# Group 0 of a fused embedding and CIN kernel: one unit unsplit, and three reorderings on ScalarE, TensorE and SyncE

## The chip, the cores and the metric

The kernel runs on one NeuronCore of one Trainium2 chip. The metric is the time of one execution on the device in microseconds (us); the time of a kernel is the median of its runs. The engines are TensorE (PE, matrix products into PSUM), VectorE (DVE), ScalarE (ACT), GpSimd (POOL) and SyncE (SP, which here only starts transfers). Each works through its own list of instructions in order, and they meet in semaphores.

## What is computed

```python
e = stack([tbl_f[ids[:, f]] for f in range(32)], axis=1)      # (512, 32, 64)
def cin(x, w0, b0, w1, b1):                                    # w: (128, channels)
    z = einsum('bhd,bfd->bhfd', x, x).reshape(B, 32*32, D)
    y = relu(einsum('bcd,oc->bod', z, w0) + b0)
    hidden, direct1 = y[:, :64], y[:, 64:]
    z = einsum('bhd,bfd->bhfd', hidden, x).reshape(B, 64*32, D)
    direct2 = relu(einsum('bcd,oc->bod', z, w1) + b1)
    return concatenate([direct1, direct2], axis=1).sum(-1)
h = concatenate([cin(e, ...), dense_ctx], axis=1)
y = relu(relu(h @ W_top1 + b_top1) @ W_top2 + b_top2) @ W_top3
```

All of it is float32. Almost all of the time goes into the two layers of the CIN: elementwise products of rows, then matrix products over them.

## The kernel before, in words

The 512 samples are worked in G = 64 groups of eight. A tile has 512 columns (8 samples x 64) and 128 partitions, a row of channels each. Work comes in units of four such tiles. Group g has one unit of layer 1, **P**, and four of layer 2, **A**, **C**, **B** and **D** (`LAYER_2`, L28). P of group g+1 is worked beside layer 2 of group g, so the order of products on VectorE is A(g), P(g+1), C(g), B(g), D(g) (`period`, L76).

A unit goes this way. VectorE multiplies rows of x (`xd` for P, A and C, `xe` for B and D, in the one buffer `xs`) by another operand (`px0` for P, and for layer 2 the PSUM tensor `hid`, whose slot 0 is the "straight" hidden rows, read by A and B, and slot 1 the "swapped" ones, read by C and D) into one of ZF = 5 slots of `zf` (`products`, L582; L616). Then `mode` (L35) says how TensorE takes it:

- whole ("F"): four float32 matrix products straight from `zf` (`main`, L717; eight records in the trace). Needs nothing of ScalarE or GpSimd.
- split ("P" or "V"): ScalarE rounds `zf` to fp32r, the high part `zh` (`high`, L434; L442); GpSimd (mode P, L377) or VectorE (mode V) subtracts it, which leaves the low part `zl` (`low`). TensorE makes eight products of the high part with the two parts of the weights (`main`, L725 and L726), and later four with the low part (`late`, L737). These are fp32r products.

P and D are whole, A of group 0 and of the odd groups below 11 too; C is split, in group 0 by mode P. Which weights are kept whole, split or both is in `WHOLE_NAMES` and `SPLIT_NAMES` (L96); they are turned and copied once, before the first group, on TensorE, ScalarE (L416 to L423) and VectorE. From group 11 on one tile of some units goes by a PSUM bank of its own (`through_bank`, L50); that is no part of this change.

What orders the work is written out by hand, one loop over the groups for each engine:

- **TensorE** (L782): main A(g), late B(g-1), main P(g+1), the small product that ends layer 1 (`tail`, L756), late A(g), then main C(g), main B(g), main D(g), late C(g).
- **ScalarE** (L513): high A(g); `high_s` and `copy_x0(g+2)` (L432, from the landed `x0` into `px0`); high C(g); `finish_2(g-1)` (relu of layer 2); high B(g); then `finish_straight(g+1)` (L466 and L467: the straight `hid` of the next group, which VectorE's A(g+1) waits for; it waits for the tail of P(g+1) and for VectorE's product of B(g), which reads the old one), `finish_dir1`, `finish_swapped`.
- **VectorE** (L658): products of A(g), in odd groups a sum (L647), products of P(g+1), a small one (`products_s`), C(g), `low_s`, B(g), D(g).
- **GpSimd** (L382): low A(g), a gather, low C(g), a gather, low B(g), a gather. The gathers (L366) bring later samples' embeddings; before the loop GpSimd issues the first 32 of them.
- **SyncE** (L337): starts `load_xt(g+2)` (L307), `load_x0(g+3)` (L301), `load_xd(g+2)` (L318), a store of gathered rows to DRAM (L284), `load_xe(g+1)` (L324). Each load is four transfers; x0 and xt bring 256 KB in all, xd and xe 1 MB each. `load_x0(k)` waits for `copy_x0(k-1)`, `load_xd(k)` for VectorE's product of C(k-2), `load_xe(k)` for that of D(k-1).

The waits name positions (`NTH`, `NTH_SPLIT`, `NTH_WHOLE`), which are counted from `mode`, so they follow a unit whose mode changes. `closing(g)` (L108) says which unit of a group is the last to be added up.

Of the kernel before, what the change touches and what calls it, by code (L numbers as in the profile page):

```python
# [13 lines left out]
P = 128  # L14
B, F, D = 512, 32, 64
# [4 lines left out]
G = B // NS  # L20
# [13 lines left out]

def mode(unit):  # L35
    name, g = unit
    if name in "PD" or unit == ("A", 0):
        return "F"
    if g == LAST and name != "A":
        return "F" if name == "B" else "V"  # L40
    if name == "A" and g < 11 and g % 2:
        return "F"
    if name == "C" and g < 11:
        return "P" if g % 2 or g == 0 else "V"
    return "P"


# [2 lines left out]
def through_bank(unit):  # L50
    name, g = unit
    return name == "P" and g > 43 or name == "C" and 11 <= g < 43 or name == "D" and 11 <= g < LAST
# [18 lines left out]
def batch_of(g):  # L71

    return len(FIRST_BATCHES) + g if g < len(LATER_BATCHES) else None
# [19 lines left out]
OWN = "PD"  # L93
NTH_OWN = {u: i + 1 for name in OWN for i, u in enumerate(v for v in BANKED if v[0] == name)}
NTH_LOW = {u: i + 1 for m in "PV" for i, u in enumerate(LOW[m])}
WHOLE_NAMES = "PABD"  # L96
SPLIT_NAMES = "ACB"


def slot(u):  # L100
    return (NTH[u] - 1) % ZF


def split_slot(u):
    return (NTH_SPLIT[u] - 1) % ZS
# [14 lines left out]
def dlrm_tower(nc, dense_ctx, ids, tables, W_top1, b_top1, W_top2, b_top2, W_top3, w0, b0, w1, b1,  # L120
               eye, out):
    with ExitStack() as ctx:
        def sb(name, shape, dt=F32):
            return ctx.enter_context(nc.sbuf_tensor(name, shape, dt))
# [10 lines left out]
        wl = sb("wl", [P, len(SPLIT_NAMES), T, P], F32R)  # L135
        wf = sb("wf", [P, len(WHOLE_NAMES), T, P])
        whB = sb("whB", [P, len(OWN), P], F32R)
# [113 lines left out]
        def _(sp):  # L251
# [38 lines left out]
            def run_of_rows(k, r):  # L290
                src = rows(k, r)
                return bass.AP(tensor=src.tensor, offset=src.offset, ap=[[P * D, F], [1, N]])


            def load_x0(k):
                if k % GC == 0:
                    sp.wait_ge(x_stored[k // GC], 16 * STORES[k // GC])
                if k >= 2:
                    sp.wait_ge(x0_ready, k - 1)
                for j in range(4):  # L300
                    sp.dma_start(x0[F * j:F * j + F], run_of_rows(k, 0)).then_inc(x0_in, 16)  # L301

            def load_xt(k):
                if k >= 2:
                    sp.wait_ge(s_mult, k)
                for j in range(4):
                    sp.dma_start(xt[F * j:F * j + F], run_of_rows(k, 16)).then_inc(xt_in, 16)  # L307
# [6 lines left out]
            def load_xd(k):  # L314
                if k >= 2:
                    sp.wait_ge(mult, NTH["C", k - 2])
                for j in (0, 2, 1, 3):
                    sp.dma_start(xd[k % 2][F * j:F * j + F], block_rows(k, j, 0)).then_inc(xd_in[k % 2], 16)  # L318

            def load_xe(k):  # L320
                if k >= 1:
                    sp.wait_ge(mult, NTH["D", k - 1])
                for j in (0, 2, 1, 3):
                    sp.dma_start(xe[F * j:F * j + F], block_rows(k, j, T)).then_inc(xe_in, 16)  # L324
# [12 lines left out]
            for g in range(G):  # L337
                if g + 2 < G:
                    load_xt(g + 2)
                if g + 3 < G:  # L340
                    load_x0(g + 3)
                if g + 2 < G:
                    load_xd(g + 2)
                if g >= 1 and batch_of(g - 1) is not None:
                    store_batch(batch_of(g - 1))
                if g + 1 < G:
                    load_xe(g + 1)
# [47 lines left out]
        def _(act):  # L395
# [20 lines left out]
            for b, name in enumerate("PACBD"):  # L416
                act.wait_ge(w_turned, b + 1)
                if name in WHOLE_NAMES:
                    act.activation(wf[:, WHOLE_NAMES.index(name)].rearrange("p t n -> p (t n)"), banks[b], ACT.Copy).then_inc(w_high, 1)
                if name in SPLIT_NAMES:  # L420
# [13 lines left out]
            def high(u):  # L434
                if mode(u) == "F":
                    return
                s, q, i = slot(u), split_slot(u), NTH_SPLIT[u]
                act.wait_ge(mult, NTH[u])
                if i > ZS:
                    act.wait_ge(used_split, i - ZS)  # L440
                first = 1 if through_bank(u) else 0
                act.activation(zh[:, q, first:T], zf[:, s, first:T], ACT.Copy).then_inc(hi, 1)  # L442
# [17 lines left out]
            def finish_straight(k):  # L460
                act.wait_ge(y1_ready, k + 1)
                if k >= 1:
                    act.wait_ge(mult, NTH["B", k - 1])
                else:
                    act.wait_ge(w_low, 5)
                act.activation(hid[0:H, 0], py1[0:H], ACT.Relu, bias=bias0[0:H]).then_inc(straight, 1)  # L466
                act.activation(hid[H:P, 0], py1[0:H], ACT.Relu, bias=bias0[0:H]).then_inc(straight, 1)  # L467
# [23 lines left out]
            def finish_2(g):  # L491
                need_used(act, closing(g))
                act.activation(py2[:, g % 2], py2[:, g % 2], ACT.Relu, bias=bias1[:]).then_inc(dir2_ready, 1)  # L493
# [19 lines left out]
            for g in range(G):  # L513
                high(("A", g))
                if g + 1 < G:
                    high_bank(("P", g + 1))
                    high_s(g + 1)
                    if g + 2 < G:
                        copy_x0(g + 2)
                high_bank(("C", g))  # L520
                high(("C", g))
                if g % GC == GC - 1:
                    place_sums_1(g // GC)
                if g >= 1:
                    finish_2(g - 1)
                high(("B", g))
                if g + 1 < G:
                    finish_straight(g + 1)
                    high_bank(("D", g))
                    finish_dir1(g + 1)  # L530
                    finish_swapped(g + 1)
# [12 lines left out]
        def _(dve):  # L544
# [18 lines left out]
            for b, name in enumerate("PACBD"):  # L563
                done += (name in WHOLE_NAMES) + (name in SPLIT_NAMES) + (name in OWN)
                if name in OWN:
# [113 lines left out]
        def _(pe):  # L679
# [15 lines left out]
            def bank(u):  # L695
                return py1[:] if u[0] == "P" else py2[:, u[1] % 2]

            def main(u):
                name, g = u
                s, y, first = slot(u), bank(u), name in "PA"  # L700
                if name == "P" and g >= 1:
                    pe.wait_ge(swapped, 3 * g)
                    pe.wait_ge(dir1_ready, g)
                if name == "A" and g >= 2:
                    pe.wait_ge(sum2_done, g - 1)
                if mode(u) == "F":
                    ends = name != "P" and closing(g) == u
                    w = WHOLE_NAMES.index(name)
                    if u != ("P", 0):
                        pe.wait_ge(mult, NTH[u])  # L710
                    first_tile = 1 if through_bank(u) else 0
                    for h in range(first_tile, T):
                        if u == ("P", 0) and h < T - 1:
                            pe.wait_ge(first_tiles, h + 1)
                        elif u == ("P", 0):
                            pe.wait_ge(mult, 1)
                        mm = pe.matmul(y, wf[:, w, h], zf[:, s, h], start=first and h == first_tile, stop=ends and h == T - 1)  # L717
                    mm.then_inc(used_whole, 1)
                else:
                    q, w = split_slot(u), SPLIT_NAMES.index(name)  # L720
                    pe.wait_ge(hi, NTH_SPLIT[u])
                    if through_bank(u):
                        pe.wait_ge(bank_hi, NTH_BANKED[u])
                    for h in range(T):
                        pe.matmul(y, wh[:, w, h], zh[:, q, h], start=first and h == 0, stop=False)  # L725
                        pe.matmul(y, wl[:, w, h], zh[:, q, h], start=False, stop=False)  # L726
# [55 lines left out]
            for g in range(G):  # L782
                main(("A", g))
                if g >= 1:
                    late_own(("D", g - 1))
                    late(("B", g - 1))
                if g + 1 < G:
                    main(("P", g + 1))
                    main_own(("P", g + 1))
                    late_own(("P", g + 1))  # L790
                    tail(g + 1)
                late(("A", g))
                main(("C", g))
                main(("B", g))
                main(("D", g))
                late(("C", g))
                main_own(("D", g))
            late(("B", LAST))
# [44 lines left out]
```

## Time and profile before

| | before |
|---|---|
| median of 3 runs | 1066.68 us (1065.88 to 1066.71) |
| profiled execution | 1065.6 us |
| its span | 1063.8 us |
| TensorE busy | 1017.4 us (96%) |
| VectorE busy | 948.7 us (89%) |
| GpSimd busy | 921.4 us (87%) |
| ScalarE busy | 772.5 us (73%) |

The span is the time from the first to the last instruction in the trace; 1.8 us of the profiled execution lie around it. Times in the views count from the start of the span. The first 62 us are the start (weights turned, first embeddings gathered, written to DRAM and loaded back), the 64 groups take the time from there to about 1038 us at some 15.2 to 16 us each, and the last layers the rest.

### The profile page before, as it was taken

Reading aid. Unit: us, or ns where it says so; the run is one execution under the profiler, and the core shown is the slowest. Engines: PE = TensorE matmul, PEld = TensorE weight load, DVE = VectorE, ACT = ScalarE, POOL = GpSimd, SP = SyncE. Lnnn points to the kernel's source line nnn. Section 1 sums busy time; section 2 is a strip of 40 time slices with the busy share of each in tenths; the row PEclk is TensorE's granted clock in tenths of the full one; section 3 lists DMA queues with packets and bytes.
Section 4 is the critical chain, followed back from the end, with each engine's and each line's share of the span. In section 5 each row is a group of like instructions: output and inputs, shape, how many; then the busy total and the mean of one; then the engine's idle time right before and its main releaser. Section 6 shows DMA issues by size and latency. Waiting matters only on the chain.

```text
span 1063.8 us, 11316 instructions
## 1 busy us (share of the span) xinstructions
PE 1017.4 (96%) x3523; PEld 662.5 (62%) x3523; DVE 948.7 (89%) x777; ACT 772.5 (73%) x908; POOL 921.4 (87%) x311
## 2 busy tenths in 40 slices
PE   2389999999999999999999999999999999999999
PEld 1146656666666666666666666666766666666663
DVE  3069999999999999999999999999999999999991
ACT  5057666678778877887788778877887787788772
POOL 6538878899999999999999999999998899899880
PEclk9999999999999999999999999999999999999999
DMA  6488788778778877887788778877766776777630
GB/s 172 97 204 193 183 194 188 179 188 192 179 180 197 185 184 181 192 194 182 182 189 189 183 177 195 192 184 172 177 168 163 168 183 163 165 181 179 162 79 0
DMA packets 140638, 183.92 MB, mean 173 GB/s; under 512 B 55633, under 2 KB 56273, under 8 KB 140450
## 3 DMA queue, kind: packets, MB, share of 16 engines
q1 hardware_dynamic: 135986, 178.93, 69.9%
q0 software_dynamic: 4096, 4.20, 2.7%
q8 instruction: 28, 0.46, 0.2%
q14 instruction: 32, 0.26, 0.1%
q10 hardware_dynamic: 496, 0.06, 0.0%
HBM read 174.66 MB, written 8.39 MB: 172 GB/s over the span
## 4 chain that ended last, share of the span: by engine, by line
PE 63%; DVE 15%; issue 9%; POOL 4%; DMA 3%; ACT 3%; SPq 2%; POOLq 0%; DVEq 0%; ACTq 0%
PE py L717 27%; PE py L737 11%; PE py L725 11%; PE py L726 11%; DVE zf L616 10%; POOL emb L366 3%; DMA xs<-x_dram 3%; DVE zlB L636 2%; DVE pzS L625 1%; ACT hid L467 1%; DVE zS L629 1%; ACT hid L466 1%; PE py L756 1%; POOL zl L377 1%; PE py L752 1%
## 5 line engine op out<-in xcount | busy, mean ns | idle before, releaser
L377 POOL TENSOR_TENSOR zl<-zf,zh 128x2048 fp32r<-128x2048 f32 x179 | 790.0, 4418 | 84.8 <-ACT zh L442 82.3
L616 DVE TENSOR_TENSOR zf<-xs,hid 128x2048 f32<-128x2048 f32 (+1 forms) x256 | 539.5, 2109 | 36.4 <-ACT hid L467 30.6
L717 PE MATMUL py<-zf,wf 128*128 128x512 f32 x936 | 423.2, 592 | 2.1 <-DVE zf L616 2.1
L442 ACT ACTIVATE zh<-zf 128x2048 fp32r<-128x2048 f32 x185 | 340.0, 1838 | 93.4 <-DVE zf L616 92.7
L725 PE MATMUL py<-zh,wh 128*128 128x512 f32 x740 | 292.3, 395 | 3.9 <-ACT zh L442 3.5
L726 PE MATMUL py<-zh,wl 128*128 128x512 f32 x740 | 290.6, 393 | 0.0
L717 PEld LDWEIGHTS py<-zf,wf 128*128 128x128 f32 x936 | 176.8, 189 | 175.1 <-issue 161.0
L737 PE MATMUL py<-zl,wh 128*128 128x512 f32 x740 | 228.7, 431 | 1.4 <-POOL zl L377 1.4
L737 PEld LDWEIGHTS py<-zl,wh 128*128 128x128 f32 x740 | 139.3, 188 | 67.5 <-issue 37.8
L725 PEld LDWEIGHTS py<-zh,wh 128*128 128x128 f32 x740 | 139.5, 188 | 42.2 <-issue 7.8
L726 PEld LDWEIGHTS py<-zh,wl 128*128 128x128 f32 x740 | 139.6, 189 | 30.0
L366 POOL DMA_INDIRECT emb<-in_tbl,idx x128 | 131.2, 1025 | 28.7 <-issue 22.9
L616 DVE TENSOR_TENSOR zf<-xs,px 128x2048 f32<-128x2048 f32 (+1 forms) x63 | 133.0, 2112 | 4.6 <-issue 4.0
L458 ACT ACTIVATE zS<-pzS 128x512 fp32r<-128x512 f32 x64 | 38.4, 599 | 86.7 <-DVE pzS L625 86.7
L493 ACT ACTIVATE py<-py,bias 128x512 f32<-128x512 f32 x64 | 42.0, 656 | 24.5 <-PE py L737 23.3
L615 DVE TENSOR_TENSOR pzB<-xs,hid 128x512 f32<-128x512 f32 x84 | 57.7, 687 | 0.0
L466 ACT ACTIVATE hid<-py,bias 64x512 f32<-64x512 f32 x64 | 41.0, 641 | 21.1 <-PE py L756 21.0
L652 DVE TENSOR_REDUCE zsum<-py 128x8 f32<-128x512 f32 x64 | 43.7, 683 | 8.4 <-ACT py L493 8.4
L636 DVE TENSOR_TENSOR zlB<-pzB,zhB 128x512 fp32r<-128x512 f32 x72 | 49.2, 684 | 0.0
L629 DVE TENSOR_TENSOR zS<-pzS,zS 64x512 fp32r<-64x512 f32 x64 | 44.5, 695 | 2.6 <-ACT zS L458 0.7
L473 ACT ACTIVATE dir<-py,bias 64x512 f32<-64x512 f32 x64 | 43.9, 686 | 1.6
L486 ACT ACTIVATE hid<-py,bias 32x512 f32<-32x512 f32 x64 | 41.1, 643 | 3.9 <-DVE zf L616 2.4
(100 smaller groups left out, 611.2 us busy)
## 6 DMA issues: line engine op xcount, KB each, us to landing
xs<-x_dram SPq DMA_DIRECT2D x512, 256.0 KB, 5.3
xs<-x_dram SPq DMA_DIRECT2D x504, 64.0 KB, 2.1
x_dram<-emb SPq DMA_DIRECT2D x66, 64.0 KB, 5.6
x_dram<-emb SPq DMA_DIRECT2D x22, 96.0 KB, 5.3
emb<-in_tbl,idx POOLq DMA_INDIRECT x128, 4.8
x_dram<-emb SPq DMA_DIRECT2D x4, 384.0 KB
xs<-in_L_rec_w SPq DMA_DIRECT2D x2, 512.0 KB, 4.4
xs<-in_L_rec_w SPq DMA_DIRECT2D x1, 1024.0 KB, 6.9
```

Source lines behind the costliest of these rows:

```text
L366: pool.indirect_dma_start(out=emb[:, c % 2, f, :], out_offset=None, in_=tables[f], in_offset=bass.IndirectOffsetOnAxis(ap=idx[:, c, f:f + ...
L377: pool.tensor_tensor(zl[:, q, first:T], zf[:, s, first:T], zh[:, q, first:T].bitcast(F32), ALU.subtract).then_inc(lo["P"], 1)
L442: act.activation(zh[:, q, first:T], zf[:, s, first:T], ACT.Copy).then_inc(hi, 1)
L466: act.activation(hid[0:H, 0], py1[0:H], ACT.Relu, bias=bias0[0:H]).then_inc(straight, 1)
L615: dve.tensor_tensor(pzB[:], left[:, 0], view(right, at, [[1, N]]), ALU.mult).then_inc(bank_mult, 1)
L616: dve.tensor_tensor(zf[:, slot(u), first:T], left[:, first:T], view(right, at, [[0, T - first], [1, N]]), ALU.mult).then_inc(mult, 1)
L629: dve.tensor_tensor(zS[H:P], pzS[H:P], zS[H:P].bitcast(F32), ALU.subtract).then_inc(s_lo, 1)
L636: dve.tensor_tensor(low_part, pzB[:], high_part.bitcast(F32), ALU.subtract).then_inc(bank_lo, 1)
L717: mm = pe.matmul(y, wf[:, w, h], zf[:, s, h], start=first and h == first_tile, stop=ends and h == T - 1)
L725: pe.matmul(y, wh[:, w, h], zh[:, q, h], start=first and h == 0, stop=False)
L726: pe.matmul(y, wl[:, w, h], zh[:, q, h], start=False, stop=False)
L737: mm = pe.matmul(y, wh[:, w, h], zl[:, q, h], start=False, stop=ends and h == T - 1)
```

## The change

In group 0 only: C is made whole, ScalarE finishes the straight `hid` of group 1 ahead of B's high part, TensorE takes D ahead of B, and SyncE starts `load_xd(2)` ahead of `load_x0(3)`. C's weights are kept whole beside their split form, for which `wf` grows by one name (2 KB in each partition) and ScalarE makes one more copy at the start.

```diff
 def mode(unit):
     name, g = unit
-    if name in "PD" or unit == ("A", 0):
+    if name in "PD" or unit in (("A", 0), ("C", 0)):
         return "F"
@@
     if name == "C" and g < 11:
-        return "P" if g % 2 or g == 0 else "V"
+        return "P" if g % 2 else "V"
@@
-WHOLE_NAMES = "PABD"
+WHOLE_NAMES = "PABCD"
@@ SyncE
                 if g + 2 < G:
                     load_xt(g + 2)
+                if g == 0:
+                    load_xd(g + 2)
                 if g + 3 < G:
                     load_x0(g + 3)
-                if g + 2 < G:
+                if 0 < g < G - 2:
                     load_xd(g + 2)
@@ ScalarE
+                if g == 0:
+                    finish_straight(1)
                 high(("B", g))
                 if g + 1 < G:
-                    finish_straight(g + 1)
+                    if g > 0:
+                        finish_straight(g + 1)
                     high_bank(("D", g))
                     finish_dir1(g + 1)
@@ TensorE
                 main(("C", g))
-                main(("B", g))
-                main(("D", g))
+                for name in "DB" if g == 0 else "BD":
+                    main((name, g))
                 late(("C", g))
```

## Rows read from the trace of the kernel before

**Rows 1.** The page: busy us (share of the span) x instructions, by engine.
```profile
PE 1017.4 (96%) x3523; PEld 662.5 (62%) x3523; DVE 948.7 (89%) x777; ACT 772.5 (73%) x908; POOL 921.4 (87%) x311
```

**Rows 2.** The chain that ended last, whole run: start us, us, what.
```profile
712.28 3.43 PE py L717 x8
717.41 1.19 DVE zf L616
```

**Rows 3.** The same chain from 44 to 110 us.
```profile
69.08 0.60 ACT px L432
69.69 1.84 ACT zh L442
...
80.51 0.93 PE py L737 x4
81.44 3.43 PE py L717 x8
...
89.46 0.23 PE py L725
```

**Rows 4.** Timeline of TensorE: start us, us, line, operation [idle before <- releaser].
```profile
62.39 7.13 PE L717 MATMUL py<-zf,wf 128*128 128x512 f32 x16 [2.15 <-DVE zf L616]
...
68.96 0.80 PE L756 MATMUL py<-zS,wS 128*128 128x512 f32 x1
...
71.57 0.50 PE L725 MATMUL py<-zh,wh 128*128 128x512 f32 x1 [1.81 <-ACT zh L442]
```

**Rows 5.** Three windows: engines' busy us (x), PEclk, DMA share, GB/s.
```profile
69.50:71.50 2.00, 0.25 (x2) 0.00 (x0) 2.00 (x2) 2.00 (x3) 0.00 (x0) 1.00 0.26 61
72.50:75.50 3.00, 3.00 (x9) 2.32 (x8) 1.19 (x2) 2.92 (x5) 3.00 (x1) 0.50 0.85 206
77.50:81.50 4.00, 4.00 (x13) 2.12 (x12) 1.91 (x2) 0.00 (x0) 4.00 (x1) 1.00 0.98 235
```

**Rows 6.** Timeline of ScalarE, groups 0 and 1.
```profile
69.62 3.70 ACT L442 ACTIVATE zh<-zf 128x2048 fp32r<-128x2048 f32 x2
...
73.22 0.63 ACT L466 ACTIVATE hid<-py,bias 64x512 f32<-64x512 f32 x1
...
73.88 0.65 ACT L467 ACTIVATE hid<-py,bias 64x512 f32<-64x512 f32 x1
...
87.77 1.91 ACT L442 ACTIVATE zh<-zf 128x2048 fp32r<-128x2048 f32 x1 [0.58 <-DVE zf L616]
```

**Rows 7.** Timeline of VectorE, groups 0 and 1.
```profile
68.34 4.49 DVE L616 TENSOR_TENSOR zf<-xs,hid 128x2048 f32<-128x2048 f32 x2
...
74.63 2.29 DVE L616 TENSOR_TENSOR zf<-xs,hid 128x2048 f32<-128x2048 f32 x1 [1.81 <-ACT hid L467]
...
76.84 0.68 DVE L647 TENSOR_REDUCE sums<-dir 128x8 f32<-128x512 f32 x1
...
79.61 2.29 DVE L616 TENSOR_TENSOR zf<-xs,px 128x2048 f32<-128x2048 f32 x1 [2.09 <-issue]
...
85.45 2.29 DVE L616 TENSOR_TENSOR zf<-xs,hid 128x2048 f32<-128x2048 f32 x1
```

**Rows 8.** Timeline of SyncE's queue: the starts for x0 of 3 and xd of 2.
```profile
69.71 1.70 SPq L301 DMA_DIRECT2D xs<-x_dram  x4
71.45 1.85 SPq L318 DMA_DIRECT2D xs<-x_dram  x4
```

**Rows 9.** Timeline of GpSimd, group 0: the low part of C.
```profile
71.60 4.58 POOL L377 TENSOR_TENSOR zl<-zf,zh 128x2048 fp32r<-128x2048 f32 x1 [26.38 <-ACT zh L442]
```

**Rows 10.** Timeline ahead of the loop: TensorE's wait, GpSimd's gather of batch 4.
```profile
41.77 5.24 PE L770 MATMUL py<-wf 128*128 128x512 f32 x8 [21.68 <-DMA emb<-in_tbl,idx]
...
44.27 0.94 POOL L366 DMA_INDIRECT emb<-in_tbl,idx  x1 [0.30 <-issue]
```

**Rows 11.** The chain ahead of the loop: the last store of batch 3.
```profile
46.72 2.16 DMA x_dram<-emb
```

**Rows 12.** Waits of VectorE, 717 to 1020 us: total us, times, longest us.
```profile
DVE pzB L615 <- DMA xs<-x_dram: 2.7, 2, 1.5
```

## The prediction

> **What bounds the kernel now.** I began with the busy times on the page: TensorE is busy for 96% of the span [rows 1], more than any other engine, so time is to be had only where TensorE stands still or runs slowly, or where the chain leaves it. The chain that ended last says where that is. It runs on TensorE's products from 77 us to 712.28 us without a break by another engine, and goes over to VectorE at 717.41 us [rows 2]. Ahead of that, in group 0, it runs over ScalarE: the copy of x0 of group 2 at 69.08, then C's high part from 69.69 to 71.53, then TensorE [rows 3]. TensorE's own timeline shows the same from its side: A and P without a pause from 62.39, the tail recorded at 68.96 for 0.80 (so ended at 69.76), and then 1.81 us of idle until C's high part is there, at 71.57 [rows 4]. The windows show a second loss behind the idle: the granted clock is 0.50 between 72.5 and 75.5 us, so 1.2 instead of 2.4 GHz, and 1.00 before and after [rows 5].
>
> How much is lost there in all comes from the ends of the tail and of group 1's A. The tail ends at 69.76 and A of group 1 ends at 81.44 + 3.43 = 84.87 [rows 3, 4], which is 15.11 us. At full speed the work between them is C main 8 x 0.23 = 1.84, B main 1.84, D 3.43, late C 0.93 and A 3.43, or 11.47 us (0.93 and 3.43 are the entries at 80.51 and 81.44, 0.23 a small product such as that at 89.46) [rows 3]. So 3.64 us are lost: the 1.8 of idle, and 1.8 of slow clock.
>
> From 82 us on TensorE has no gap, so what it gains by then is carried on. I take it to be carried to the end, also behind 717 us: VectorE's work there hangs on semaphores of the other engines and not on a date, and everything in it moves together.
>
> **C unsplit.** TensorE needs C's product only, and not its high part. That product is made directly ahead of the small `low_s` and B's at 68.34 [rows 7], so it is ready at about 67.6 while TensorE gets to it at 69.76. The idle goes. The price is 3.43 for a whole unit instead of 1.84 + 0.93 = 2.77, so 0.66 us more of TensorE. ScalarE loses a high part of 1.84 [rows 3], GpSimd a low part of 4.58 [rows 9]; neither is the bound here.
>
> **D ahead of B on TensorE.** C then ends at 69.76 + 3.43 = 73.19. D's product ends at 68.34 + 4.49 = 72.83 [rows 7], 0.36 before; D ends at 76.62. If B came first, it would need its high part. ScalarE now does the straight hid first: it needs B's product (half-way through the entry of 4.49, so at 70.6) and the tail (69.76), starts at 70.65, and by the two durations of 0.63 and 0.65 [rows 6] ends at 71.95. B's high part follows and ends at about 73.85, 0.7 us after C's end at 73.19. The order D, B hides that. B main ends at 76.62 + 1.84 = 78.46. Late C is gone. A of group 1 ends at 78.46 + 3.43 = 81.89.
>
> So the sum of TensorE's part is 84.87 - 81.89 = **2.98 us** (3.64 lost before, less 0.66).
>
> **Straight hid first on ScalarE.** VectorE's A of group 1 waited 1.81 us for it and began at 74.63 [rows 7]. It now begins when D's product is over, at 72.9, and ends 2.21 later at 75.1. TensorE wants it at 78.46, so this is not on the path by itself; it starts the row of what follows. What is queued behind the moved step on ScalarE is B's high part (73.85 instead of 73.32, wanted at 76.62) and then `finish_dir1` and `finish_swapped`, which end at about 76.5. Of GpSimd, B's low part now starts at 73.9 and takes 4.58 [rows 9], so it ends at 78.5; TensorE wants it at 81.89.
>
> **xd of 2 ahead of x0 of 3.** VectorE's P of group 2 began at 79.61 after 2.09 us with no releaser named [rows 7]. The sum ahead of it had ended at 77.5, and what it needs beside that is xd of group 2, whose first transfer started at 71.45 [rows 8]; from there to its use are 8.16 us. The load waits only for C's product, so it now starts at 67.6. At the same 8.16 us it is used at 75.8, which is just when VectorE is through with A and the sum (75.1 + 0.68). I expect it sooner, as 256 KB of x0 no longer lie ahead of it and the DMA engines were at 0.26 of their time between 69.5 and 71.5 us [rows 5]. The four starts take 1.85 us [rows 8], to 69.5, and x0 of 3 has to wait for the copy that ends at 69.68 anyway: it starts at 69.7 as before, but its data come behind the 1 MB. Its use is the copy behind group 1's small product, at about 79.5; it has ten us. xe of 1 waits for D's product (72.83) and starts then; before, it followed xd's starts, at 71.45 + 1.85 = 73.3, so it is 0.5 us sooner.
>
> Then VectorE's chain in group 1 is: P of 2 at 75.8, B of 1 another 85.45 - 79.61 = 5.84 later [rows 7], at 81.65, its product ended at 83.9 and its high part, by 1.91 [rows 6], at 85.8. TensorE wants that at 91.30 - 2.98 = 88.3 (before, C began at 89.46 and took 1.84). The lead is 2.5 us. Without this reordering P would stay at 79.6, the high part at 87.77 + 1.91 = 89.68 [rows 6], and TensorE would stand for 1.4 us. So this part brings nothing by itself, and saves 1.4 of the 2.98.
>
> Here a rule speaks against the simple reading of the queue. The Trainium skill says, in "DMA: Bandwidth & Descriptors", section "Two DMAs through the same engine are not ordered", that in one queue descriptors start in order but are pipelined, and that nothing orders transfers across the 16 engines. By it xe of 1 may run beside xd of 2 and delay it, up to the case without any gain from the reordering. The rows leave this open: the DMA engines were at 0.98 from 77.5 to 81.5 us [rows 5], when parts of both loads were under way.
>
> **The start.** One more copy of weights on ScalarE, about 0.6 us, lies under the 21.68 us in which TensorE waits for gathers [rows 10]; without that cover it would cost its 0.6. On GpSimd the second gather of batch 4 stood behind C's low part. With that gone it is issued right behind the first one (44.27, 0.94 each) [rows 10], at about 45.5, beside the last stores to DRAM that the chain runs through (46.72, 2.16 us) [rows 11]. Bounds: 0 if it slips into the gaps, 2.2 if the stores had to wait until it is through, as long as a store takes. It is 32 KB on another queue than the stores', so I take 0.1, near the lower end.
>
> **Sum:** 2.98 - 0.1 = 2.9 us. Against the profiled execution, 1065.6 - 2.9 = 1062.7 us; the median of the runs is 1.1 us above that execution, so the forecast for the median is **1063.8 us**. A measurement of this kernel can tell about 0.2%, 2.1 us, from no change; 2.9 is 0.27%.
>
> **Rivals.**
>
> 1. The slow clock stays. The granted clock fell after 1.81 us of idle [rows 4, 5], but 2.15 us of idle lie ahead of A at 62.39 [rows 4] and stay as they are; the clock held through the 16 records behind it (7.13 us, so 0.43 us apart as in 3.43 for eight). If the dip is still there, it falls on C and D and costs its 1.8: gain 1.1, time 1065.6. The Trainium skill, "TensorE: Matmul & The Clock Gate", "Part 1: The HAM clock gate", has the clock follow how busy TensorE has lately been and its change vary from run to run, so by that rule a dip could also come of the earlier gap. For my forecast: with the change there is no idle from 62.39 on. Chance 0.08.
> 2. A transfer takes back the gain. xd of 2 or xe of 1 does not come sooner, and TensorE waits in group 1 for B's high part: gain 2.98 - 1.4 = 1.6, time 1065.1. For it: xe of 1 starts only 0.5 us sooner. Against: 2.5 us of lead. Chance 0.12.
> 3. Slower. From 717 us on VectorE sets the pace and has no slack; a load that lands late there is paid in full. Twice it was: 2.7 us, the longest 1.5 [rows 12]. The change starts loads in another order and moves all phases by 3 us. If four more loads out of some twenty groups come late, each by 1.35, the kernel loses 5.4 - 2.9 = 2.5, time 1069.2; from the third late one on (4.05) it is slower than before, from the fourth by over 0.2%. Against it: the order of loads differs in group 0 only. Chance 0.04. The same in the other direction, those 2.7 us going away, gives 1061.1; chance 0.03.
> 4. The gather at the start hits the stores in full: gain 0.8, time 1065.9. Chance 0.03.
>
> That the change doesn't do what it says I rule out nearly: the waits are counted from the modes.
>
> **How the numbers follow.** The forecast has the remaining 0.70. Its own range is 1063.1 to 1064.6, by the 0.4 or so to which the runs agree and some tenths of the sum. The range for 8 in 10 takes in rivals 1 and 2: 1062.8 to 1065.6. Faster by over 0.2% means a gain over 2.1 us: nearly all of the forecast's cases (0.67), the better end of rival 2 (0.02) and the lucky case (0.03), 0.72. Slower by over 0.2% only by rival 3: 0.04. Within 0.2%: the rest, 0.24.
>
> **What would show it.** In the trace after: TensorE at L717 without an idle entry from 62.4 on, through C and D of group 0 to about 76.6; PEclk at 1.00 in the window 72.5 to 75.5; A of group 1 ended at about 81.9; VectorE's A of 1 at 72.9 and P of 2 at about 75.8, with no wait for a transfer over some tenths; and in the later groups the same times less 3 us, such as the chain leaving TensorE at about 714 us. An idle entry of TensorE before B of group 1 speaks for rival 2, a PEclk of 0.5 near 73 us for rival 1, more than 3 us of VectorE waiting for transfers after 714 us for rival 3, and a first A later than 62.4 for rival 4.

## The result and the profile after

The changed kernel takes 1062.28 us as the median of 6 runs (1060.93 to 1062.75), the kernel before 1066.28 in 6 runs beside it (1064.68 to 1066.94): ratio 0.9968, 95% interval 0.9955 to 0.9980. The forecast was 1063.8 us, 2.9 us less than before; the two medians differ by 4.0 us, the ratio says 3.4, and its interval 2.1 to 4.8 us less. In absolute terms the median lies 0.5 us below the prediction's range of 1062.8 to 1065.6. That range counted from the 1066.68 us of the first three runs, and the kernel before measured 1066.28 in the six; 1066.68 x 0.9968 is 1063.3, which lies inside. The profiled execution took 1062.44 us with a span of 1060.6 us, against 1065.6 and 1063.8, so 3.2 us less.

The page of the changed kernel, busy times and the granted clock by slices: TensorE is busy for as long as before (1017.4), in a span that is 3.2 us shorter.

```profile
PE 1017.3 (96%) x3519; PEld 661.0 (62%) x3519; DVE 947.4 (89%) x777; ACT 770.0 (73%) x908; POOL 917.9 (87%) x310
...
PEclk9999999999999999999999999999999999999999
```

The chain of the changed kernel from 44 to 110 us (start, duration, what) in place of [rows 3]: from A of group 0 at 62.16 everything is TensorE's; the 16 records from 69.53 are C and D, and A of group 1 ends at 78.43 + 3.43 = 81.86.

```profile
62.16 7.13 PE py L723 x16
...
69.53 7.06 PE py L723 x16
...
78.43 3.43 PE py L723 x8
```

TensorE's timeline, where [rows 4] had 1.81 us of idle ahead of C: there is no idle entry, C and D begin 0.63 us after the tail.

```profile
62.16 7.13 PE L723 MATMUL py<-zf,wf 128*128 128x512 f32 x16 [1.23 <-DVE zf L622]
68.73 0.80 PE L762 MATMUL py<-zS,wS 128*128 128x512 f32 x1
69.36 7.22 PE L723 MATMUL py<-zf,wf 128*128 128x512 f32 x16
...
78.27 3.60 PE L723 MATMUL py<-zf,wf 128*128 128x512 f32 x8
```

Three windows, as [rows 5] (the last three columns are PEclk, DMA share, GB/s): the clock is at 1.00 where it was at 0.50, and the DMA engines are at work between 69.5 and 71.5 us.

```profile
69.50:71.50 2.00, 2.00 (x6) 0.82 (x5) 2.00 (x2) 0.75 (x2) 0.00 (x0) 1.00 0.89 210
72.50:75.50 3.00, 3.00 (x8) 1.25 (x7) 3.00 (x3) 2.92 (x4) 1.54 (x1) 1.00 1.05 239
77.50:81.50 4.00, 4.00 (x14) 2.13 (x12) 3.80 (x4) 2.06 (x3) 2.94 (x3) 1.00 0.73 194
```

ScalarE, VectorE, SyncE and GpSimd, as [rows 6 to 10]. ScalarE makes the straight hid at 70.72, then B's high part. VectorE's entry of 6.68 us holds B, D and A of group 1 in one, without the wait of 1.81; P of group 2 starts at 75.54 without a wait, 7.93 us behind the first start of its load. In the eight traces in which P of 2 does wait, from 7.94 us (g1) to 9.22 us (f2) lie between the two, against the 8.16 us of the prediction. SyncE starts xd of 2 at 67.61, x0 of 3 at 69.48, xe of 1 at 72.85. GpSimd issues the second gather of batch 4 at 45.58.

```profile
70.72 0.65 ACT L469 ACTIVATE hid<-py,bias 64x512 f32<-64x512 f32 x1 [1.27 <-DVE zf L622]
71.40 0.65 ACT L470 ACTIVATE hid<-py,bias 64x512 f32<-64x512 f32 x1
71.98 1.90 ACT L445 ACTIVATE zh<-zf 128x2048 fp32r<-128x2048 f32 x1
...
83.96 1.91 ACT L445 ACTIVATE zh<-zf 128x2048 fp32r<-128x2048 f32 x1 [0.47 <-DVE zf L622]
```

```profile
68.34 6.68 DVE L622 TENSOR_TENSOR zf<-xs,hid 128x2048 f32<-128x2048 f32 x3
74.94 0.68 DVE L653 TENSOR_REDUCE sums<-dir 128x8 f32<-128x512 f32 x1
75.54 2.28 DVE L622 TENSOR_TENSOR zf<-xs,px 128x2048 f32<-128x2048 f32 x1
...
81.64 2.29 DVE L622 TENSOR_TENSOR zf<-xs,hid 128x2048 f32<-128x2048 f32 x1 [0.30 <-DMA xs<-x_dram]
```

```profile
67.61 1.74 SPq L318 DMA_DIRECT2D xs<-x_dram  x4
69.48 1.86 SPq L301 DMA_DIRECT2D xs<-x_dram  x4
72.85 1.74 SPq L324 DMA_DIRECT2D xs<-x_dram  x4
```

```profile
45.58 0.94 POOL L369 DMA_INDIRECT emb<-in_tbl,idx  x1 [0.30 <-issue]
73.96 4.57 POOL L380 TENSOR_TENSOR zl<-zf,zh 128x2048 fp32r<-128x2048 f32 x1 [27.44 <-ACT zh L445]
```

The chain over the whole run leaves TensorE at 714.39 instead of 717.41 [rows 2], and the waits of VectorE behind it for transfers are what they were [rows 12].

```profile
709.26 3.43 PE py L723 x8
714.39 1.19 DVE zf L622
```

```profile
DVE pzB L621 <- DMA xs<-x_dram: 2.8, 2, 1.8
```

### The profile page after: what moved, and what is told of

It reads as the page before. It is cut to its first block, busy times and chain, and to the rows that moved or that the text cites. A ratio compares the mean times of both kernels' runs of the same rounds, so it can differ in the third digit from the quotient of the medians.

```text
span 1060.6 us, 11306 instructions
## 1 busy us (share of the span) xinstructions
PE 1017.3 (96%) x3519; PEld 661.0 (62%) x3519; DVE 947.4 (89%) x777; ACT 770.0 (73%) x908; POOL 917.9 (87%) x310
## 4 chain that ended last, share of the span: by engine, by line
PE 64%; DVE 16%; issue 9%; ACT 4%; DMA 2%; ACTq 2%; SPq 1%; POOL 1%; POOLq 0%; DVEq 0%
PE py L723 28%; DVE zf L622 11%; PE py L743 11%; PE py L731 10%; PE py L732 10%; DVE zlB L642 2%; DMA xs<-x_dram 1%; ACTq L502 1%; DVE pzS L631 1%; ACT hid L470 1%; DVE zS L635 1%; ACT hid L469 1%; PE py L762 1%; POOL zl L380 1%; DMA xs<-in_L_rec_w 1%
## 5 line engine op out<-in xcount | busy, mean ns | idle before, releaser
L445 ACT ACTIVATE zh<-zf 128x1536 fp32r<-128x1536 f32 (+1 forms) x184 | 338.2, 1838 | 94.5 <-DVE zf L622 90.5
L631 DVE TENSOR_TENSOR pzS<-xs,px 128x512 f32<-128x512 f32 x63 | 43.4, 689 | 0.0
```

What stands on the lines that cost most here:

```text
L631: dve.tensor_tensor(pzS[:], left, right, ALU.mult).then_inc(s_mult, 1)
```

## The experiments

To read them, three stretches of the profiled executions are told apart. The tail (the small product that ends layer 1, one for each group) marks the groups on TensorE's timeline. From the tail of group 4 to that of group 45 the traces all take 625.5 us (625.7 in e4, 626.1 in the second trace of the changed kernel); what differs is the first groups and the last ones.

| kernel | A of 0 starts | tail of 2 | tail of 4 | tail of 4 less A of 0 | P of 2 on VectorE | slow clock (0.50) from |
|---|---|---|---|---|---|---|
| before | 62.39 | 88.67 | 120.09 | 57.70 | 79.61 | 72 |
| changed | 62.16 | 85.66 | 117.07 | 54.91 | 75.54 | none |
| changed, second trace (f1) | 62.41 | 85.98 | 117.40 | 54.99 | 75.86 | none |
| e1: C unsplit alone | 62.60 | 87.02 | 120.82 | 58.22 | 81.16 | none |
| e2: C unsplit and xd | 62.83 | 87.83 | 119.24 | 56.41 | 77.18 | 63 |
| e3: without xd | 63.28 | 89.57 | 120.99 | 57.71 | 79.93 | 62.5 |
| e4: without D first | 63.37 | 88.46 | 119.87 | 56.50 | 76.98 | 64 |
| e5: xd alone | 63.04 | 87.63 | 119.05 | 56.01 | 77.93 | none |
| e6: three orders, C split | 62.56 | 87.23 | 118.65 | 56.09 | 76.03 | none |
| e7: C's idle filled | 62.60 | 88.65 | 120.07 | 57.47 | 80.15 | 63 |
| f2: changed, A's idle filled | 62.37 | 85.67 | 117.09 | 54.72 | 76.84 | none |
| f3: before, A's idle filled | 62.78 | 89.11 | 120.56 | 57.78 | 80.89 | 73 |
| f4: as f2, without xd | 62.34 | 85.79 | 119.67 | 57.33 | 79.92 | none |
| g1: before, both filled | 62.03 | 86.40 | 118.27 | 56.24 | 78.63 | none |

The slow clock meant in the last column is the one in the first groups. It turned out to be there in some executions and not in others, and the mean granted clock of each timed run tells which: without it the mean is 1.000 or 0.989, with it 0.997 or 0.998, or 0.986 or 0.987. What lies between 1.000 and 0.989 is another stretch at 0.50, of some 24 us, ahead of the groups; of the kernels with and without it, g1 and f2 (busy us of TensorE, x, PEclk, DMA share, GB/s):

```profile
24.00:27.00 3.00, 0.00 (x0) 1.00 0.66 128
```

```profile
24.00:27.00 3.00, 0.00 (x0) 0.50 0.68 136
```

Of 112 runs of the kernel before, 50 have the slow clock in the first groups. Of these, 39 have a mean of 0.986 or 0.987, and 11 one of 0.997 or 0.998. In the six traces that have it, the first pair of values goes with a slow clock behind the idle ahead of A (e2, e3, e4, e7), the second with one behind C's idle (before, f3). So the place that the forecast had read from one trace is, by this sign, the rarer one. The sign is not a proof: e2 and e3, which have no idle ahead of C, have one run each at 0.998, and f3, which has none ahead of A, one at 0.987.

**e1: only C unsplit.**

```diff
-    if name in "PD" or unit == ("A", 0):
+    if name in "PD" or unit in (("A", 0), ("C", 0)):
         return "F"
-        return "P" if g % 2 or g == 0 else "V"
+        return "P" if g % 2 else "V"
-WHOLE_NAMES = "PABD"
+WHOLE_NAMES = "PABCD"
```

> Only C of group 0 made whole; the three orders are as before. Theory (my account of the forecast): TensorE goes on from the tail into C without idle; B's high part now follows the copy of x0 and VectorE's product of B (70.6), so it ends at about 72.5, before C ends at 73.2, and neither straight-first nor D-first is needed. A of group 1 ends 2.98 us sooner than before (about 81.9 us in the trace), but P of group 2 still waits for xd until 79.6, and TensorE then idles about 1.4 us before B of group 1: gain 1.6 us, ratio 0.9985. Rival (the gain is spread over the parts, the straight hid being the wait that counts): VectorE's A of group 1 starts only at about 73.9, A of group 1 on TensorE is late, and the gain at its end is under 2 us and under 1 us in all.

Measured: 1066.03 us against 1065.98, ratio 1.0001 (0.9992 to 1.0010). No gain at all, less than even the 1.6 us of the theory. VectorE's P of group 2 and the idle entries of TensorE in this kernel:

```profile
81.16 2.29 DVE L616 TENSOR_TENSOR zf<-xs,px 128x2048 f32<-128x2048 f32 x1 [3.78 <-issue]
```

```profile
83.59 3.67 PE L717 MATMUL py<-zf,wf 128*128 128x512 f32 x8 [0.45 <-DVE zf L616]
...
88.24 0.50 PE L725 MATMUL py<-zh,wh 128*128 128x512 f32 x1 [0.72 <-ACT zh L442]
...
91.29 0.50 PE L725 MATMUL py<-zh,wh 128*128 128x512 f32 x1 [0.93 <-ACT zh L442]
...
104.37 1.20 PE L737 MATMUL py<-zl,wh 128*128 128x512 f32 x4 [0.21 <-POOL zl L377]
```

P of 2 waits for its load until 81.16, not 79.6 (in this execution the starts on SyncE were later too), and TensorE then waits four times. The tail of 2 came 1.65 us sooner than before, the tail of 4 at 120.82, 0.73 later. In this execution what C unsplit saves is all given back to a load.

**e2: C unsplit and xd ahead of x0.** As e1, and

```diff
+                if g == 0:
+                    load_xd(g + 2)
                 if g + 3 < G:
                     load_x0(g + 3)
-                if g + 2 < G:
+                if 0 < g < G - 2:
                     load_xd(g + 2)
```

> C of group 0 whole and xd of 2 ahead of x0 of 3; ScalarE's and TensorE's orders as before. Theory: these two parts make the whole gain: A of group 1 ends at about 81.9, P of group 2 starts on VectorE at about 76.8, no idle entry on TensorE in group 1: gain 3.0 us, as much as the whole change, within 0.5 us of it. Rival (the straight hid first or D first has a part): over 1 us less gain than the whole change.

Measured: 1063.15 us, ratio 0.9974 (0.9965 to 0.9983), 2.8 us less than before. The whole change has 0.9968 and 0.9969; the intervals overlap, and half a microsecond between them can't be excluded. No idle entry in group 1. But the trace has the slow clock behind the idle ahead of A of group 0, in a place where the trace before did not have it. The windows (busy, x, PEclk, DMA share, GB/s), and TensorE's A and P of group 0 in it, 8.83 instead of 7.13 us:

```profile
60.00:63.00 3.00, 0.61 (x3) 1.00 1.07 240
63.00:66.00 3.00, 3.00 (x5) 0.56 1.05 231
66.00:69.00 3.00, 3.00 (x8) 0.87 1.00 228
```

```profile
62.83 8.83 PE L719 MATMUL py<-zf,wf 128*128 128x512 f32 x16 [2.39 <-DVE zf L618]
```

Less these 1.7 us, tail of 4 less A of 0 is 54.7, as in the changed kernel. The times show the same cost: the four runs of e2 with the slow clock have a median of 1064.62 us, the seven without it 1063.05, which is 2.2 us less than the 14 runs of the kernel before without it on the same chip (1065.26).

**e3: without the reordering on SyncE.** The change with load_xd where it was.

> The change without the reordering on SyncE. Theory: A of group 1 still ends 3.0 us sooner, P of group 2 starts at 79.6 as before, B's high part of group 1 is late and TensorE idles about 1.4 us ahead of B of group 1: gain 1.6 us, as in the kernel with C unsplit alone. Rival (the load would have come in time anyway, xe of 1 sets the pace): full gain of 3.0 us. Second rival: the delay is felt in later groups too and grows past 1.4: gain under 1 us.

Measured: 1066.22 us, ratio 0.9994 (0.9983 to 1.0004). The trace could not judge the theory: P of 2 was late as foreseen (79.93), but a slow clock from 62.5 us on, to 69.3, twice as long as in the other traces, had put TensorE 3 us back (10.12 instead of 7.13 us for the first 16 records), so that it met no late product.

```profile
63.28 10.12 PE L720 MATMUL py<-zf,wf 128*128 128x512 f32 x16 [2.82 <-DVE zf L619]
```

By the median of all runs the gain of the change is gone but for 0.6 us. Six of the eleven runs have the slow clock (median 1066.34); the five without it have a median of 1063.77, 1.5 us less than the kernel before without it, near the 1.6 of the theory. Five runs that spread over 3.8 us can't decide this; f4 below has it with twelve.

**e4: without D ahead of B.**

```diff
-                for name in "DB" if g == 0 else "BD":
-                    main((name, g))
+                main(("B", g))
+                main(("D", g))
```

> The change without D ahead of B on TensorE. Theory: B's high part, behind the straight hid on ScalarE, ends at about 73.9 and C at about 73.0 to 73.2, so TensorE idles 0.7 to 0.9 us before B of group 0: A of group 1 ends 0.7 to 0.9 us later than in the changed kernel, gain about 2.2 us. The clock stays at 1.00, since the idle is short. Rival: the idle is enough to bring the slow clock back: gain under 1 us.

Measured: 1064.04 us, ratio 0.9980 (0.9971 to 0.9989), so about 2.1 us less than before, as the theory has it (2.2); the difference to the whole change, about 1.2 us, is near the foreseen 0.7 to 0.9 but inside what two intervals leave. The trace again has the slow clock, from 64 us on, which hides the wait that was to be seen: B's high part is there when C ends.

**e5: xd ahead of x0 alone.** The SyncE part of e2 on the kernel before.

> Only xd of 2 ahead of x0 of 3; everything else as before. Theory: P of group 2 starts on VectorE at about 77.5, right after the sum, instead of 79.6, but TensorE has no wait there before the change: gain 0 (within 0.3 us in the trace at the end of A of group 1, ratio 1.000). Rival (the load was a bound of its own): gain over 1 us.

Measured: 1065.34 us against 1065.12, ratio 0.9998 (0.9985 to 1.0011). No gain in the time. Its trace has no slow clock, and TensorE still waits 1.66 us for C's high part: the tail of 4 is 56.01 us behind A, 1.7 sooner than before. That is the size of the slow clock which it lacks. Whether the sooner xd has a part in it is not shown, as no trace of the kernel before without the slow clock was taken.

**e6: the three orders, C still split.**

> All three orders of the change, but C of group 0 stays split. Theory: C's high part still ends at 71.5 and TensorE idles 1.8 us before it and runs slowly behind it: gain 0 to 0.3 us, no more. Rival (the orders carry a part of the gain): over 1 us.

Measured: 1064.65 us, ratio 0.9998 (0.9986 to 1.0010). The idle ahead of C is 1.77 us as before. Its trace has no slow clock either, and its tail of 4 is 56.09 us behind A, as in e5. By the times the orders without the unsplit unit bring nothing, as the theory has it.

**e7: C's idle filled.**

```diff
                 late(("A", g))
+                if g == 0:
+                    warm_up(2, pzB[:])
                 main(("C", g))
```

> The kernel before, with two float32 products of weights into the unused PSUM bank pzB on TensorE between the tail and C of group 0 (1.7 us of work that is thrown away, in the 1.8 us of idle). Theory (the idle of 1.8 us before C brings the slow clock, which costs 1.8 us): PEclk stays at 1.00 from 72.5 to 75.5 us, C's first product starts at about 71.6 as before, A of group 1 ends about 1.8 us sooner (83.0), and of that 1.5 to 1.8 us arrive at the end, as B of group 1 then waits some tenths for its high part. Rival (the dip comes of the idle before A at 62.4 or of its own): PEclk 0.50 there as before, gain 0.

Measured: 1066.57 us against 1065.12, ratio 1.0017 (1.0006 to 1.0028): slower. In the trace the slow clock was not at 72 us but at 63, behind the idle ahead of A, so that the tail came late (70.87), the two products were no longer hidden and C began at 72.82, 0.9 us behind the end of its high part (70.10 + 1.85 = 71.95). That doesn't explain the loss in the times, as the five runs without a slow clock have a median of 1066.57 us too.

**The second series** was made for the slow clock and for the late load without it. First the changed kernel once more.

> The changed kernel once more, beside the kernel before on the same chip. The runs so far show a half-clock stretch of 3.4 us (1.7 us lost) in the first groups in some executions only, in either of two places: behind the idle ahead of A of group 0 (63 us) or behind the idle ahead of C (72 us). Theory: the change removes 1.8 us of idle for 0.66 us of work (1.15 us) in every execution, and the dip at 72 us only where it occurred. So executions without a dip (mean clock 0.989 or 1.000) differ by about 1.2 us between the two kernels, and the medians of all by 1.2 to 2.5. Rival (the forecast as it stood: 3 us, whatever the clock): about 3 us in the executions without a dip too.

Measured: 1063.37 us in 12 runs against 1066.28 in 35, ratio 0.9969 (0.9959 to 0.9979). By the mean clock none of the 12 has the slow clock in the first groups, and 20 of the 35 of the kernel before have. But the 15 without it have a median of 1066.39 us, the 20 with it 1066.26. So the rival is right on this chip: the gain is about 3 us in the executions without it as well, and not the 1.2 us of the theory. On the chip of e1 to e4 the two kinds of executions do differ (e2 above), so the share of the clock in the gain is not settled.

**f2, f3, f4: the idle ahead of A of group 0 filled**, in the changed kernel, in the kernel before, and in the changed kernel without the reordering on SyncE.

```diff
-            warm_up(3, pzB[:])
+            warm_up(5, pzB[:])
```

> The changed kernel with five thrown-away products instead of three between the tail and A of group 0, so that the idle there (1.2 to 2.8 us) is down to some tenths. Theory (a dip needs idle of TensorE some us before it): no dip from 50 us on in any execution, mean clock 0.989 or 1.000 only; the median as that of the changed kernel's executions without a dip, within 0.5 us. Rival (a dip comes of its own): mean clocks of 0.987 or 0.998 in some runs as often as without.

> The kernel before with the same five thrown-away products. The idle of 1.8 us ahead of C of group 0 stays. Theory: a dip, where there is one, is now always the one behind C's idle (72 us); the distance to the changed kernel with five products is 1.15 us without and 2.9 us with it. Rival (only both idles together bring the dip): no dip at all, distance 1.2 us throughout.

> The changed kernel without SyncE's reordering, with five thrown-away products, so that no dip ahead of C hides a late load (in the first look of that kernel a dip at 63 us had made TensorE 3 us late). Theory: P of group 2 starts on VectorE at 79.6 to 81.2 instead of 75.5, TensorE waits in groups 1 and 2, and the gain is 1.4 to 3.3 us less than that of the changed kernel with five products. Rival: the reordering on SyncE brings nothing without a dip either (within 0.5 us).

Measured on one chip, beside 1066.28 for before: f2 1063.54 (ratio 0.9978, 0.9969 to 0.9987), f3 1066.22 (1.0005, 0.9993 to 1.0017), f4 1066.92 (1.0010, 0.9998 to 1.0021). No run of f2 and f4 has the slow clock (0 of 24), 3 of 12 of f3 have. In f3's trace it sits behind C's idle, as the theory has it; windows with PEclk in the third place from the end:

```profile
69.00:72.00 3.00, 1.18 (x5) 1.00 0.25 56
72.00:75.00 3.00, 3.00 (x9) 0.63 0.79 175
75.00:78.00 3.00, 3.00 (x11) 0.80 1.01 216
```

f4 is the clean form of e3. VectorE's P of groups 2 and 3, and the idle entries of TensorE:

```profile
79.92 2.29 DVE L619 TENSOR_TENSOR zf<-xs,px 128x2048 f32<-128x2048 f32 x1 [4.33 <-issue]
...
94.63 2.29 DVE L619 TENSOR_TENSOR zf<-xs,px 128x2048 f32<-128x2048 f32 x1 [1.03 <-DMA xs<-x_dram]
```

```profile
87.01 0.50 PE L728 MATMUL py<-zh,wh 128*128 128x512 f32 x1 [0.58 <-ACT zh L442]
...
90.06 0.50 PE L728 MATMUL py<-zh,wh 128*128 128x512 f32 x1 [0.94 <-ACT zh L442]
...
103.14 1.20 PE L740 MATMUL py<-zl,wh 128*128 128x512 f32 x4 [0.20 <-POOL zl L377]
```

In f2 the same P of 2. The entry names TensorE, but the load is the likelier cause: it is 9.22 us behind its first start (67.62) here, and VectorE stood 1.2 us for it, which no product of TensorE felt:

```profile
76.84 2.29 DVE L621 TENSOR_TENSOR zf<-xs,px 128x2048 f32<-128x2048 f32 x1 [1.21 <-PE py L722]
```

Both kernels reach the tail of group 2 at the same time (85.79 and 85.67). f4 then needs 16.35 us to the next tail and 17.53 to the one behind it, f2 14.44 and 16.98: 2.5 us lost. The waits for the high parts of C and B of group 1 (0.58 and 0.94) make 1.5 us, near the 1.4 that were foreseen. The rest comes since the next loads hang on the late products: xd of 3 is started at 86.45 instead of 83.37, P of 3 begins at 94.63 instead of 91.37 (it waits for its transfer in both, 1.03 and 0.85 us), and A's low part of group 2 is late for TensorE (0.20). The medians differ by 3.4 us, those of e1 and e2 by 2.9. So the reordering on SyncE is worth 2.5 to 3.4 us once C is unsplit, and by the times nothing without that (e5).

**g1: the kernel before with both idle stretches filled**, the diffs of e7 and f3 together.

> The kernel before with both idle stretches of TensorE filled with thrown-away products (five ahead of A of group 0, two ahead of C), so that no slow clock can hide anything; all orders and modes as before. Revised theory (two chains end together in groups 1 to 3: TensorE's own, and the late load of xd of 2; the slow clock only covers the second): no dip; the tail of group 2 at about 87.0 us instead of 88.7, but then idle of TensorE in groups 1 and 2 before C and B of 1 to 2.5 us, and the tail of group 4 at 119.5 to 120.8 us, as with the dip (120.1): ratio 1.000 within 0.001. Rival (the dip costs its 1.7 us): no idle in group 1, tail of group 4 at about 118.4, gain 1.7 us, ratio 0.9984.

Measured: 1066.13 us against 1064.84, ratio 1.0018 (1.0007 to 1.0028), slower as e7. No run of the 12 has the slow clock. In the trace, TensorE has one idle entry up to the tail of 4, of 0.17 us, and P of 2 is at 78.63, a microsecond sooner than before:

```profile
101.82 1.19 PE L737 MATMUL py<-zl,wh 128*128 128x512 f32 x4 [0.17 <-POOL zl L377]
```

```profile
78.63 2.29 DVE L616 TENSOR_TENSOR zf<-xs,px 128x2048 f32<-128x2048 f32 x1 [1.87 <-PE py L717]
```

The tail of 4 is at 118.27, 56.24 behind A, 1.5 us sooner than before. So neither the revised theory (119.5 or later) nor the rival (118.4, and the gain at the end) holds: in the trace 1.5 of the slow clock's 1.7 us are won, in the times none.

## Why the prediction was right, and where it was not

**The sum on TensorE.** A of group 1 was to end at 81.89 and ends at 81.86; D's end, foreseen at 76.62, is at 76.59. The gain in the profiled pair there is 3.01 us, foreseen 2.98, and arrives at the end as 3.2. VectorE's P of 2 was to start at 75.8 (it started at 75.54), B of 1 at 81.65 (81.64), its high part to end at 85.8 (83.96 + 1.91 = 85.87). xe of group 1 was the narrowest: VectorE waited 0.30 us for it in the first trace and not in the second.

**The start** cost nothing that can be seen: A of 0 began at 62.16 and 62.41 in two traces, 62.39 before.

**To the end.** The step "I take it to be carried to the end" held: with the tails of groups 11 and 45 at 225.78 and 742.59 against 228.80 and 745.61, the lead is 3.02 us at both.

**A mis-sized term: the load of xd.** The forecast gave SyncE's part 1.4 us, from one wait in group 1. Measured it is 2.5 us in the first groups (f4 against f2) and 2.9 to 3.4 in the medians, as the late product also makes the next loads late. Rival 2, with a gain of 1.6 us left, was too kind: without SyncE's part little or nothing is left (e1 1.0001, e3 0.9994, f4 1.0010). Beside it the orders on ScalarE and TensorE were taken to be needed together, and e4 (0.9980) points the same way. That C unsplit and xd alone do all but at most some tenths (e2) follows from the same sums, since B's high part is ready at 73.2 when ScalarE takes it first (71.27 + 1.92 in e1), but the prediction did not work it out.

**The slow clock.** The forecast took the 1.8 us behind C's idle as lost in every execution. This is the step that did not hold. The runs show it in 50 of 112, and by the mean clocks mostly in a place where the trace before did not have it, behind the 2.15 us ahead of A [rows 4]; that idle is what rival 1 had pointed at, and in e2, e3, e4 and e7 the slow clock was there. That the trace from which the forecast was made had it behind C's idle, and that of the changed kernel had none, is in part luck. The rule of the Trainium skill that it leaned on ("TensorE: Matmul & The Clock Gate", "Part 1: The HAM clock gate": the clock follows how busy TensorE has been, and varies from run to run) agrees with this: the stretch is in none of the 36 runs of the kernels without either idle (f2, f4, g1). It is in none of the 18 runs of the changed kernel either (6 and 12), which keeps 1.2 to 1.8 us of idle ahead of A. But e1 to e4, which keep that idle and have none ahead of C, have it in 15 of 44 runs. Why the changed kernel was spared is not shown.

So the forecast of 2.9 us was right for the profiled pair term by term. For the medians part of its reason is open: the executions of the kernel before without the slow clock should be 1.5 to 1.7 us faster than those with it. They are 1.2 us faster on one chip (1065.26 against 1066.46, 14 and 19 runs) and 0.3, 0.6 and -0.1 us on the three others (1064.86 against 1065.18, 1064.82 against 1065.37, 1066.39 against 1066.26). A late load of xd would take it back where P of 2 is as late as in e1 and f4; that is argued, and in g1 it did not. What the spread of 2 to 7 us between runs of one kernel hides here can't be told from single traces. The profiled executions show where most of it lies: from the tail of 45 to the last tail they take from 275.8 us (e2) to 278.3 (e1), and the changed kernel and the kernel before are alike in that (276.06 and 276.16).

**Other rivals.** Rival 2 (a transfer takes back the gain) is what happens without SyncE's part, and not with it. Whether xe of 1, under way beside xd of 2, delays it, no run tells: P of 2 waited for nothing in the changed kernel and 1.2 us in f2, and neither reached TensorE. Rival 3 did not come: 2.8 us of waits for transfers against 2.7. Rival 4 did not either.

**A cheaper way that no run tried.** The chain before reaches C's high part by way of x0 of group 2: ScalarE stood 3.06 us for that load, then copied it, and only then took C, whose product had been there since about 67.6. The row of the chain that [rows 3] begins behind:

```profile
60.10 8.96 DMA xs<-x_dram
```

With C's high part ahead of the copy it would end at about 67.6 + 1.84 = 69.5, before the tail ends at 69.76, and C could stay split: the idle would go without the 0.66 us more of products. This is an estimate from the rows of the trace before. The copy, and x0 of 3 behind it, would come later, so it too would want xd of 2 moved ahead. The experiments show that a whole C takes the idle away, and not that it is the best way to do so.

## What to carry to other kernels

Where two chains end nearly together, here TensorE's own and the load of the group after next, neither change shows alone (ratios 1.0001 and 0.9998) and both together do (0.9974). (The first and the last of these were measured on one chip, the second on another.) So before a part is dropped as useless, work out what comes late next once the first wait is gone, and count that a late product also delays the loads that wait for it. And a loss that a trace shows once, such as a slow clock, needs several traces or the clocks of the timed runs before it goes into a sum.

## What was not expected of the hardware

The two kernels with two thrown-away products in C's idle were slower by 0.17% and 0.18% (e7 and g1, intervals clear of 1), also in their runs without a slow clock (medians 1066.57 and 1066.13), though g1's trace shows C starting sooner (70.81) and the first groups faster than before. Behind the tail of 45 their traces take 276.95 and 277.16 us to the last tail against 276.16 before, but other kernels spread as far (275.8 to 278.3). Two more such products ahead of A did nothing of the kind (f3 1.0005, f2 near f1). What takes this time was not found.
